# A message-passing kernel: which engine fetches which edge columns of a pass, and in what units

## The reference

```python
# L0, and twice in L3: a sum
out = jax.ops.segment_sum(H[src] * norm[:, None], dst, num_segments=n)
...
# L2, four times: a maximum
diff = x[src] - x[dst]
msg = diff @ tw.T + tb + phi[dst]
agg = jax.ops.segment_max(msg, dst, num_segments=x.shape[0])
```

## Time and profile before

| | |
|---|---|
| time, median of 3 runs | 9439.49 us (9435.47 to 9441.98) |
| the profiled execution's own time | 9444.14 us |
| its span, first to last instruction | 9442.3 us |
| busy: POOL / DVE / ACT / PE | 6987.7 / 3654.1 / 3485.0 / 1819.4 us |
| indirect gathers of the seven passes (L1035) | 5502, 944 ns mean |

### The profile page before, as it was taken

The page is one execution under the profiler, slowest core; times in us unless marked ns, Lnnn a source line. Parts: engine busy times, 40 slices in busy tenths (PEclk is TensorE's granted clock), DMA queues, the critical chain, the costliest instruction groups (busy, mean ns, idle before and its releaser), DMA issues. The chain is left out here.

```text
span 9442.3 us, 137452 instructions
## 1 busy us (share of the span) xinstructions
PE 1819.4 (19%) x9607; PEld 1531.1 (16%) x9607; DVE 3654.1 (39%) x20408; ACT 3485.0 (37%) x23810; POOL 6987.7 (74%) x6815
## 2 busy tenths in 40 slices
PE   2000057788884000020002000020002000020000
PEld 1000046777774000010001000010001000010000
DVE  4333344444443333333333333333334333333333
ACT  4444221111114444334442444334442444324441
POOL 5777668888883777777777777777776777777777
PEclk6555567777777555565556555565555555555555
DMA  6444535555553333333333333333334333333333
GB/s 214 161 159 158 190 79 77 77 77 77 75 72 111 108 108 112 110 108 108 113 111 111 111 109 108 113 105 112 108 110 138 103 117 111 109 108 110 108 112 128
DMA packets 483882, 1071.04 MB, mean 113 GB/s; under 512 B 162484, under 2 KB 293278, under 8 KB 428104
## 3 DMA queue, kind: packets, MB, share of 16 engines
q0 software_dynamic: 310432, 442.95, 21.5%
q1 hardware_dynamic: 169557, 619.06, 17.8%
q10 hardware_dynamic: 2940, 1.00, 0.1%
HBM read 511.83 MB, written 559.14 MB: 113 GB/s over the span
## 5 line engine op out<-in xcount | busy, mean ns | idle before, releaser
L1035 POOL DMA_INDIRECT WORK<-table,S x5502 | 5194.3, 944 | 1923.2 <-issue 1689.0
L1071 DVE COPY FE<-XF 128x4 uint8 x9856 | 1311.1, 190 | 3271.9 <-issue 1824.8
L1114 ACT COPY FE<-XF 128x4 uint8 x20608 | 2101.3, 191 | 1104.6 <-issue 1092.0
L1134 ACT COPY WORK<-psum 128x512 f32<-128x512 f32 (+1 forms) x1456 | 846.3, 581 | 2874.1 <-DVE psum L1089 2864.6
L1304 POOL DMA_INDIRECT acc<-TOT,stage x832 | 1301.3, 1564 | 274.6 <-issue 209.7
L1089 DVE SCALAR_TENSOR_TENSOR psum<-psum,RESET,WORK 128x128 f32<-128x128 f32 x3320 | 1189.1, 358 | 493.3 <-DMA WORK<-table,S 426.8
L1154 PE MATMUL psum<-ident,FE 128*128 128x128 f32 x238 | 106.5, 447 | 6110.0 <-ACT FE L1114 4714.0
L1089 DVE SCALAR_TENSOR_TENSOR psum<-psum,KEEP,WORK 128x128 f32<-128x128 f32 x2490 | 896.9, 360 | 639.9 <-DMA WORK<-table,S 278.8
L1154 PEld LDWEIGHTS psum<-ident,FE 128*128 128x128 f32 x238 | 43.3, 182 | 6172.5 <-issue 5903.0
L1438 ACT COPY TOT<-psum 128x512 f32<-128x512 f32 x208 | 121.9, 586 | 1250.2 <-DMA acc<-TOT,stage 1245.0
L1509 DVE SCALAR_TENSOR_TENSOR BASE<-psum,WEIGHT,BASE 128x128 f32<-128x128 f32 x832 | 234.1, 344 | 761.9 <-PE psum L1379 761.8
(11 more groups left out here) (255 smaller groups left out, 2540.4 us busy)
## 6 DMA issues: line engine op xcount, KB each, us to landing
run_rows<-WORK SPq DMA_DIRECT2D x357, 1024.0 KB, 4.2
WORK<-table SPq DMA_DIRECT2D x10752, 0.5 KB
WORK<-table,S POOLq DMA_INDIRECT x5502, 2.6
fill_rows<-BASE SPq DMA_DIRECT2D x52, 1024.0 KB, 6.8
WORK<-fill_rows SPq DMA_DIRECT2D x104, 512.0 KB, 3.7
table<-TF SPq DMA_DIRECT2D x56, 384.0 KB
WORK<-carry_rows SPq DMA_DIRECT2D x49, 384.0 KB, 6.6
acc<-TOT,stage POOLq DMA_INDIRECT x832, 3.3
```

Of the source, the lines that this page charges most:

```text
L1035: pool.indirect_dma_start(RING_T[:, b * WIDE + k, :], None, table, table_row(table, INDEX[:, t:t + 1]))\
L1071: i = dve.tensor_copy(PICKED[:, s, e:e + 1].bitcast(u8), TT[:, ds(held_rows["dve"][e % 32], 4)])
L1114: i = act.copy(PICKED[:, j % 2, e:e + 1].bitcast(u8), TT[:, ds(held_rows["act"][e % 32], 4)])
L1134: act.copy(RING_T[:, t % SPAN:t % SPAN + n, :], CHAINED[:, t % PSUM_COLS:t % PSUM_COLS + n, :])\
```

## The change

ScalarE takes 30 columns a pass, VectorE 24, SyncE 15; GpSimd keeps 763. All three work in units of 32 edges, each with one TENSOR_LOAD ahead. ScalarE does a unit in 5 of every 8 quads. VectorE does one ahead of every eighth reduction. SyncE's columns are the last but one of their blocks, three blocks apart and once in sixteen blocks four; a half is issued behind the store of block c-3 and the other behind that of c-2. The wait for the store of block c-4 stays ahead of the first half. The load of the residual moves from block 48 to block 50, and the set-up makes the offsets of several columns with one instruction.

```diff
-BY_ACT = [t for t in range(60, 772, 32)]
-BY_DVE = [t for t in range(108, 772, 64)]
-BY_SP = [t for t in range(84, 800, 64)]
+UNIT = 32
+UNITS = P // UNIT
+TT_LAST = 800
+
+ACT_QUADS = [q for q in range(TT_LAST // QUAD) if q % 8 in (0, 1, 3, 4, 6)]
+BY_ACT = [t for t in (QUAD * (q + 5) for q in ACT_QUADS[UNITS - 1::UNITS]) if t < TT_LAST]
+DVE_STEPS = list(range(4, TT_LAST, 8))
+BY_DVE = [t for t in (QUAD * (s // QUAD + 5) + 1 for s in DVE_STEPS[UNITS - 1::UNITS]) if t < TT_LAST]
+SP_BLOCKS = [c for c in range(3, TT_LAST // WIDE) if c % 16 in (3, 6, 9, 12, 0)]
+BY_SP = [WIDE * c + WIDE - 2 for c in SP_BLOCKS]
...
-X_BLOCK = 48
-STEP_EDGES = 2
+X_BLOCK = 50
...
                 def pick_edges(t):
...
+                    if t not in DVE_STEPS:
+                        return
+                    j, unit = divmod(DVE_STEPS.index(t), UNITS)
+                    if j >= len(BY_DVE):
+                        return
+                    if unit == 0:
+                        wait(dve, tt_copied, len(tt_quads) if j == 0 else 0)
+                        wait(dve, off_turned, FROM_TT.index(BY_DVE[j - 2]) + 1 if j > 1 else 0)
+                    rows = row_offsets(mybir.EngineType.DVE, len(BY_ACT) + j, unit)
+                    for e in range(UNIT):
+                        i = dve.tensor_copy(PICKED[:, 2 + j % 2, unit * UNIT + e:unit * UNIT + e + 1].bitcast(u8),
+                                            TT[:, ds(rows[e], 4)])
+                    if unit == UNITS - 1:
+                        i.then_inc(built_v, 1)
...
                         c = col // WIDE
-                        k = after - max(c - RING, -1)
-                        parts_of = ((0, 64), (64, 64)) if c >= RING else ((0, 128),)
-                        if not 0 <= k < len(parts_of):
+                        half = after - (c - RING + 1)
+                        if half not in (0, 1):
                             continue
-                        first, n = parts_of[k]
-                        if k == 0:
-                            wait(sp, stored[c % RING], c // RING * 16)
-                        for a in range(first, first + n, 32):
-                            rows = row_offsets(mybir.EngineType.SP, len(BY_ACT) + len(BY_DVE) + j, a, 32, 4 * F)
-                            for e in range(32):
+                        wait(sp, stored[c % RING], c // RING * 16 if half == 0 else 0)
+                        for unit in range(half * UNITS // 2, (half + 1) * UNITS // 2):
+                            rows = row_offsets(mybir.EngineType.SP, len(AWAY) - len(BY_SP) + j, unit, 4 * F)
+                            for e in range(UNIT):
```

More of the change, by code:

```diff
@@ L46 @@
 PSUM_COLS = 24
-BY_ACT = [t for t in range(60, 772, 32)]
-BY_DVE = [t for t in range(108, 772, 64)]
-BY_SP = [t for t in range(84, 800, 64)]
+UNIT = 32
[7 more added lines that the diff above has]
+BY_SP = [WIDE * c + WIDE - 2 for c in SP_BLOCKS]
 FROM_TT = sorted(BY_ACT + BY_DVE)
 AWAY = BY_ACT + BY_DVE + BY_SP
-EDGES = 16
-X_BLOCK = 48
-STEP_EDGES = 2
+X_BLOCK = 50
 COUNT = T // WIDE
@@ L632, in _ @@
                                   ALU.is_equal).then_inc(hot, 1)
-                for k, (t, size) in enumerate([(t, 4) for t in BY_ACT + BY_DVE] + [(t, 4 * F) for t in BY_SP]):
-                    i = dve.tensor_single_scalar(AWAY_F[:, k:k + 1], SRCF[:, t:t + 1], float(size), ALU.mult)
+                k = 0
+                for cols_of, period, size in ((BY_ACT, 5, 4), (BY_DVE, 1, 4), (BY_SP, 5, 4 * F)):
+                    n = len(cols_of)
+                    for r in range(period):
+                        own = cols_of[r::period]
+                        assert own == list(range(own[0], own[-1] + 1, own[1] - own[0]))
+                        i = dve.tensor_single_scalar(AWAY_F[:, k + r:k + n:period],
+                                                     SRCF[:, own[0]:own[-1] + 1:own[1] - own[0]],
+                                                     float(size), ALU.mult)
+                    k += n
                 i.then_inc(hot, 1)
@@ L995, in _, with row_offsets @@
                 wait(sp, x_parked, 16 * NG if x_loads == 1 else 0)
-        def row_offsets(engine, k, first, n, size=4):
+        def row_offsets(engine, k, unit, size=4):
             return nc.values_load_multi_w_load_instructions(
-                ROWB[k:k + 1, first:first + n], engines=[engine], min_val=0, max_val=(N_PAD - 1) * size,
+                ROWB[k:k + 1, unit * UNIT:(unit + 1) * UNIT], engines=[engine], min_val=0,
+                max_val=(N_PAD - 1) * size,
                 skip_runtime_bounds_check_because="the offsets are made of node numbers below N_PAD")[1]
@@ L1024, in passing @@
             tt_quads = pieces(NT, QUAD) if FROM_TT else []
-            held_rows = {}
             def pool_part(pool):
@@ L1104, in pick_edges @@
                 def pick_edges(q):
[L1105 to L1117, removed]
+                    if q not in ACT_QUADS:
+                        return
+                    j, unit = divmod(ACT_QUADS.index(q), UNITS)
+                    if j >= len(BY_ACT):
+                        return
+                    if unit == 0:
+                        wait(act, off_turned, FROM_TT.index(BY_ACT[j - 2]) + 1 if j > 1 else 0)
+                    rows = row_offsets(mybir.EngineType.Activation, j, unit)
+                    for e in range(UNIT):
+                        i = act.copy(PICKED[:, j % 2, unit * UNIT + e:unit * UNIT + e + 1].bitcast(u8),
+                                     TT[:, ds(rows[e], 4)])
+                    if unit == UNITS - 1:
+                        i.then_inc(built_a, 1)
                 for q, (t, n) in enumerate(tt_quads):
@@ L1173, in fetch @@
                         c = col // WIDE
-                        k = after - max(c - RING, -1)
-                        parts_of = ((0, 64), (64, 64)) if c >= RING else ((0, 128),)
-                        if not 0 <= k < len(parts_of):
+                        half = after - (c - RING + 1)
+                        if half not in (0, 1):
                             continue
-                        first, n = parts_of[k]
-                        if k == 0:
-                            wait(sp, stored[c % RING], c // RING * 16)
-                        for a in range(first, first + n, 32):
-                            rows = row_offsets(mybir.EngineType.SP, len(BY_ACT) + len(BY_DVE) + j, a, 32, 4 * F)
-                            for e in range(32):
-                                sp.dma_start(RING_T[a + e:a + e + 1, col % SPAN, :].bitcast(u8),
+                        wait(sp, stored[c % RING], c // RING * 16 if half == 0 else 0)
+                        for unit in range(half * UNITS // 2, (half + 1) * UNITS // 2):
+                            rows = row_offsets(mybir.EngineType.SP, len(AWAY) - len(BY_SP) + j, unit, 4 * F)
+                            for e in range(UNIT):
+                                p = unit * UNIT + e
+                                sp.dma_start(RING_T[p:p + 1, col % SPAN, :].bitcast(u8),
                                              flat_table[:, ds(rows[e], 4 * F)]).then_inc(fetched[j % 2], 16)
@@ L1188, in sp_part @@
                     sp.wait_ge(blanked, 1)
-                fetch(-1)
                 for c in range(COUNT):
```

## The result

The changed kernel takes 9669.62 us in the median of 4 runs (9667.77 to 9677.4), the kernel before 9438.62 (9435.47 to 9441.98, also 4). The ratio is 1.0246, with a 95% interval of 1.0229 to 1.0264: 2.5% slower. The profiled execution took 9677.4 us, its span is 9675.7; the difference that has to be explained is 9677.4 - 9444.14 = 233.3 us.

What follows compares the result with a forecast made beforehand. GpSimd's gathers bound six passes before; after the change SyncE's fetch loop was to decide. 9444.1 + 114 (six passes) + 61 (first pass) - 2 (set-up) = 9617, stated as a 9610 us median, 1.8% slower; range 9420 to 9870.

Steps and rivals of the forecast that it cites:

- What bounds, and what is lost: GpSimd's gathers bound six passes before; after, SyncE's loop outlasts 55.0 us of gathers per three blocks; 1.8% slower.
- fast case: Rival, 8%: SyncE's loop stays under 55.0 us, so the whole 201 us of saved gathers comes; 9240 us.
- SyncE's halves and the loop: Two fetch halves of 27.6 us, plus 1.3 and 1.8 through the column to its block's store: 58.3 us per three blocks.
- The step up to 60.5: Later passes' three-block loop, taken between 58.3 (SyncE alone) and 62.3 us, nearer the upper.
- a store's shadow: VectorE's and ScalarE's offset loads run longer beside SyncE's stores; on VectorE 2 to 4.6 us, twice in three blocks.
- The first store: Start of each pass: first block store 27.4 us after the first gather.
- The six passes: Later passes: gathers end at 1001 us instead of 981.3, 19 later each; +114 us.
- The first pass: Pass that also stores zeros: loop 64.7 us, four blocks 82, gathers end at 1071 against 1010.3; +61 us.
- The rest: After a pass's last gathers: unchanged; the moved residual load costs at most some 10 us in three passes.
- VectorE isn't the bound: Rival, 16%: VectorE's blocks exceed 18.3 us and bound the passes; kernel 10,150 us, or 10,800 with 0.19 a copy.
- GpSimd isn't held up: Rival, 5%: 1664 more VectorE copies a pass each hold a gather's work for 0.16 us; 266 us a pass, 11,000.
- The set-up's 2 us: Set-up: 46 small instructions in 2.7 us become 11; -2 us at most.

Runs made afterwards that it cites:

- Spread copies: Changed kernel with each VectorE unit of 32 copies laid as four behind each of eight reductions; 9569.66 us.
- halved ones: Changed kernel with 17 VectorE copies a unit instead of 32, so half the edges of its columns get other data; 9570.61 us.
- SyncE alone: Kernel before with only SyncE's new columns and halves and the moved residual load, VectorE's old pairs of copies kept; 9529.76 us against 9441.53.
- SyncE as before: Changed kernel with SyncE's part undone (12 columns four blocks apart, halves behind stores c-4 and c-3); 9290.83 us against 9439.49 for the kernel before.

## Why the prediction was right, and where not

*What bounds, and what is lost:* right. GpSimd waits for stores of the ring, every 60 us, behind SyncE's fetches; halving those gave 196 of the 201 us that the prediction's fast case had.

*SyncE's halves and the loop.* 27.6 forecast, 28.0 to 28.3 measured; from the last fetch to the store 3.1 forecast, mostly about 3 measured. Together 59.3 to 59.6 instead of 58.3. The step up to 60.5 was argued from loads on VectorE in a store's shadow; there it was wrong. Spread copies, halved ones and the old pairs all left the three-block interval at 58 to 60, and VectorE stood idle for 8.15 us in the one shown. The shadow costs where a whole block is reduced: four blocks took 76.0 to 79.3, forecast 76, and 73.4 where VectorE is light.

*The first store* was taken at 27.4 us into a pass. It came at 8612.56 - 8578.64 = 33.9. The diff shows why, and the prediction overlooked it: VectorE's first unit now stands ahead of column 4's reduction and waits for the table that ScalarE copies into SBUF at the start of a pass. VectorE's timeline and ScalarE's, last pass:

```profile
8584.98 1.54 DVE L1102 SCALAR_TENSOR_TENSOR psum<-psum,KEEP,WORK 128x128 f32<-128x128 f32 x4 [6.57 <-DMA WORK<-table,S]
8594.20 1.24 DVE L1084 COPY FE<-XF 128x4 uint8 x11 [7.67 <-issue]
```

```profile
8585.94 5.83 ACT L1135 COPY XF<-psum 128x512 f32<-128x512 f32 x7 [0.29 <-PE psum L1155]
```

The table's last copy ends at 8591.77, the load and the first picked edge follow. Before, VectorE's first pick came some 55 us into the pass. That this wait is the cause was read, not tried by itself; with VectorE's and ScalarE's old work (SyncE alone) the first fetch came 7.0 us earlier.

*The six passes:* +125 measured, +114 forecast. The last first half was forecast at 921 us into a pass; in the last pass its fetches begin at 926.3, so about 921.6 for its store. The start 6.5 late and four blocks 2 longer made up for eleven intervals 1 shorter: a sum that came out better than its terms, by luck.

*The first pass* is the mis-sized term: +95 measured, +61 forecast. The loop was 66.5 us on average instead of 64.7, four blocks 85.0 instead of 82, the start 34.4 instead of 27.4: 11 x 1.8 + 3 x 3.0 + 7.0 = 36, about the 34 that are missing. And its reason was wrong in part: the prediction took SyncE alone at 61.8 and charged 2.9 for VectorE and ScalarE. With VectorE's old pairs (SyncE alone) the loop was already 65.8 to 67.1. The term that failed is SyncE's first half, charged with 28.4 because the wait for its store was taken to be gone, that store being a block older now. So it is where the last column was four blocks back (27.9 to 28.2). Where it was three back, SyncE comes late from its fetches and issues two zero stores and two block stores in a row; the store of block c-4 has not landed then, and SyncE waits for it again, 35.3 us in the eleven first halves. Its load behind the zeros takes longer, too. They took 30.5 to 33.8, 32.6 on average; the one shown goes from the last store at 294.09 to the last fetch at 304.58 + 23.34 = 327.92, 33.8 us.

*The rest:* the prediction left what follows the last gathers of a pass unchanged; it took 13 us more, and no run looked for the cause. SyncE alone and SyncE as before lose under 1 us there.

*The rivals.* VectorE isn't the bound: 17.5 us a block against 17.7 forecast, though it costs some 14 us a pass. GpSimd isn't held up: with 3072 copies a pass, in runs of 32, gathers stay at 944 ns, and SyncE as before lets all 766 pass in 956 us. The Trainium skill, SBUF — State Buffer, section SBUF: two separate sides, says that a VectorE operation in a two-port mode locks GpSimd out of the port pair that they share; no run here shows that lock, since in none did the gathers' mean move by more than 2 ns, and whether these copies use that mode no run tells. The set-up's 2 us did not show.

## What to carry to other kernels

Before work is moved to an engine that looks idle, add up its own list over the period in which it now has to repeat: SyncE showed no busy time at all, and its 56 us of issuing against 55 of gathers turned a gain into a loss: with SyncE's part left as it was, the same change is 1.6% faster. Then look which waits move with the moved work, at the start of a loop too, and which wait that was thought to be gone comes back when an engine runs late. And lay small copies between instructions of a dependent chain, where they hide, not in front of them.

## What was not expected of the hardware

An offset load takes longer with stores in flight: on SyncE some 2.2 us alone, 3.4 to 4.3 just behind a 1 MB block store, and 5.9 to 6.6 behind a zero store and a block store (second halves of the first pass); behind two of each it was no longer than that, 5.3 to 6.2. Copies in a run of 32 follow each other every 0.106 us, though each holds a register instruction and takes about 0.2 us by itself. And one engine's few microseconds of lateness cost others nothing until the ring ran dry: with SyncE's columns every four blocks, halves of the same 28 us left no wait at all in the later passes.
